# A new order for the convolutions and the gated block behind a shifted-window attention: finer split steps, more buffers, one core

## The reference, cut to what matters

```
x = x + attention(gn(x))      # shifted 7x7 windows, 8 heads, softmax
x = x + binary_conv(gn(x))    # sign(input) (*) sign(kernel), 3x3, times box-summed |gn(x)|, plus bias
x = x + ternary_conv(gn(x))   # full-precision input (*) sign(kernel), 3x3
x = x + gated(gn(x)):
    xb, z = split(x_flat @ W_in)            # 128 + 128 channels
    u = silu(causal_conv4(xb) + conv_b)     # per channel, along the 784 tokens of an image
    out = (4 * u * silu(z)) @ W_out
```

## Time and profile before

| | |
|---|---|
| median of 3 runs | 215.12 us (214.6 to 215.54) |
| the profiled execution | 215.54 us, its span 213.7 us |
| PE busy | 200.5 us (94%) |
| DVE, ACT, POOL busy | 152.2, 138.8, 91.7 us |
| attention | to about 126.8 us |
| conv stage | 126.8 to 174.3 us |
| gated block | 174.3 to 208.6 us, then its last steps and the store |

### The profile page before, as it was taken

How to read it: one execution, slowest core, us unless ns; L and a number is a source line. 1 busy time by engine, 2 the same in 40 slices (tenths; PEclk the granted TensorE clock), 3 DMA queues, 4 the chain that set the end, 5 groups by cost and what they waited for, 6 DMA issues and landing times.

```text
span 213.7 us, 6850 instructions
## 1 busy us (share of the span) xinstructions
PE 200.5 (94%) x2767; PEld 140.6 (66%) x2767; DVE 152.2 (71%) x316; ACT 138.8 (65%) x294; POOL 91.7 (43%) x103
## 2 busy tenths in 40 slices
PE   7888999999999999999999998999689899899994
PEld 2456788888888878888788875665456564545441
DVE  3585699977886868878769764989797861625543
ACT  2347697779776987788878662188445455876631
POOL 0359999730325199322792019487435410100000
PEclk9999999999999999999999999999999999999999
DMA  6970000000000000000000000001343300002022
GB/s 208 440 294 3 3 3 3 3 3 3 5 3 3 0 5 3 3 3 3 2 3 3 5 3 0 0 5 41 79 100 94 86 0 3 0 0 75 14 108 104
DMA packets 4382, 9.16 MB, mean 43 GB/s; under 512 B 641, under 2 KB 3201, under 8 KB 4225
## 3 DMA queue, kind: packets, MB, share of 16 engines
q1 hardware_dynamic: 4208, 8.41, 11.9%
q10 hardware_dynamic: 144, 0.34, 0.4%
HBM read 5.03 MB, written 1.61 MB: 31 GB/s over the span
## 4 chain that ended last, share of the span: by engine, by line
PE 71%; DVE 8%; ACT 7%; DMA 4%; issue 4%; POOL 3%; SPq 1%; ACTq 0%; DVEq 0%; POOLq 0%
PE turned L691 12%; PE outs L711 11%; PE scores L680 10%; PE scores L893 5%; PE scores L894 4%; PE qkv L651 4%; PE qkv L661 4%; PE scores L793 4%; PE turned L921 3%; PE outs L733 2%; DMA xw<-xw_in 2%; PE turned L839 2%; DMA p<-parts 2%; PE scores L911 2%; ACT pt L460 2%
## 5 line engine op out<-in xcount | busy, mean ns | idle before, releaser
L1014 DVE TENSOR_REDUCE mx<-scores 113x16 f32<-113x784 f32 x32 | 30.9, 965 | 8.3 <-PE scores L680 8.1
L691 PE MATMUL turned<-cst,d 113*113 113x113 f32 x256 | 33.3, 273 | 0.9 <-DVE d L1019 0.9
L691 PEld LDWEIGHTS turned<-cst,d 113*113 113x113 f32 x256 | 27.8, 178 | 8.5 <-issue 7.1
L460 ACT ACTIVATE pt<-turned 113x392 f32<-113x392 f32 x64 | 28.4, 495 | 7.1 <-PE turned L691 5.9
L206 POOL TENSOR_TENSOR kex<-ks,cst 128x784 f32<-128x784 f32 (+1 forms) x16 | 23.5, 1472 | 20.9 <-ACT ks L439 20.8
L1019 DVE TENSOR_TENSOR d<-scores,mx 113x784 f32<-113x784 f32 x32 | 31.2, 976 | 1.1
L711 PEld LDWEIGHTS outs<-vsb,pt 113*49 113x49 f32 x1024 | 26.1, 125 | 6.1 <-issue 2.9
L430 ACT ACTIVATE scores<-rel 113x784 f32<-113x784 f32 x32 | 26.1, 817 | 5.1 <-DMA rel<-rel_in 3.9
L711 PE MATMUL outs<-vsb,pt 113*49 113x18 f32 x1024 | 29.2, 199 | 0.0
L283 POOL TENSOR_TENSOR rstd<-ve,mhalf 128x1 f32<-128x1 f32 (+1 forms) x15 | 8.7, 577 | 46.7 <-DVE ve L980 46.6
L680 PE MATMUL scores<-kex,qs 32*49 32x196 f32 x512 | 28.2, 332 | 0.0
(11 more groups left out here) (118 smaller groups left out, 359.1 us busy)
## 6 DMA issues: line engine op xcount, KB each, us to landing
p<-parts SPq DMA_DIRECT2D x14, 112.5 KB, 2.2
x<-x_in SPq DMA_DIRECT2D x1, 1568.0 KB, 9.8
out<-res SPq DMA_DIRECT2D x8, 196.0 KB, 1.9
xw<-xw_in SPq DMA_DIRECT2D x2, 392.0 KB, 4.9
xw<-xw_in SPq DMA_DIRECT2D x1, 784.0 KB, 6.7
ker<-ker_in SPq DMA_DIRECT2D x2, 288.0 KB, 10.1
p3x<-parts SPq DMA_DIRECT2D x8, 60.0 KB, 2.0
late<-late_in SPq DMA_DIRECT2D x1, 417.0 KB, 10.8
```

The costliest lines, as they stand in the source:

```text
L460: act.activation(pt[0:WK, k % 2, j].rearrange("p n (w t) -> p n w t", w=2), ps_t[j][0:WK, :].rearrange("p (n w t) -> p n w t", n=4, w=2)[: ...
L691: mm = pe.transpose(ps_t[j][0:WK, n * P:n * P + WK], d[0:WK, k % 2, h:h + 2, :].rearrange("p a b -> p (a b)")[:, 0:WK], ident[0:WK, 0:WK])
L1014: dve.tensor_reduce(top, sc, AXX, ALU.max).then_inc(max_done, 1)
```

## The change

- On PE the last values, projections, channel sums and `conv1` steps behind the attention stand in another order; `channel_sums(3, *)` now stands ahead of the first `conv2_stacked`, and `conv2` is written out in its three steps.
- `split_a` is cut into `first_part` and `whole` (the bfloat16 part first, then `xf`); `split_b` into `second_part` and `place_second`. SP's sends are a list, with both first parts (g = 0, 1) ahead of the third part of 0.
- Conv2 has semaphores of its own (`conv2_done`, `x2_done`).
- The last three `mix` steps are `mix(col(3, 1..3))` behind `conv2_third(3)`, in the spare columns of another bank (`late_mix`); before it was two, and `mix(col(3, 1))` stood ahead of `conv2(3)`.
- `tap_weights` moves from the conv stage into step R = 8 of the attention on DVE. It also makes `wo4`, four times `wo`, so that the product is a plain multiply.
- A one-column Silu, and with it the table load, stands in ACT's program right behind the attention loop.
- `xs` holds all 4 groups, `su` and `sz` 8 halves. `yy` and `res` lie over the dead tiles `kex` and `xw`. The expands use banks 2 and 3, the gate branches 6, 7, 0 and 1 by turns.
- The gated block is interleaved by single steps on PE, ACT and DVE.
- `ON_POOL` and `BY_TAPS` are empty, so the branches for them are dead code.

The core of the diff:

```
         SHF = 3
-        xs = sb("xs", [P, 2, 2, SHF + TOK])
-        su = sb("su", [P, 4, HALF])
-        sz = sb("sz", [P, 4, HALF])
-        yy = sb("yy", [P, 4, HALF])
+        xs = sb("xs", [P, NG, 2, SHF + TOK])
+        wo4 = sb("wo4", [P, C])
+        su = sb("su", [P, 8, HALF])
+        sz = sb("sz", [P, 8, HALF])
...
+            def send_part(part, g):
                 s = g % 2
                 if g >= 2:
-                    sp.wait_ge(conv_done, 2 * NG + 2 * (g - 1))
+                    sp.wait_ge(conv2_done, 2 * (g - 1))
...
+            act.wait_ge(ld_late, 16)
+            act.activation(warm[:], warm[:], ACT.Silu).then_inc(warm_set, 1)
             evac_ka(0)
             evac_att(NR - 1)
...
             absolutes(NG - 1)
-            split_a(0)
             evac_ka(4)
+            first_part(0)
+            whole(0)
             evac_ka(5)
-            split_b(0)
-            split_a(1)
+            first_part(1)
+            whole(1)
+            second_part(0)
+            place_second()
...
+            channel_sums(0, 0)
+            values(NP - 1)
             conv1(0, 0)
-            values(NP - 1)
             project(NR - 2)
-            channel_sums(0, 0)
             gather(NR - 1)
+            channel_sums(0, 1)
+            channel_sums(1, 0)
+            project(NR - 1)
             conv1(0, 1)
...
+            conv2_third(3)
+            mix(col(3, 1), 1, nth(3, 1), late_mix)
+            gate_branch(0)
+            gate_branch(1)
+            mix(col(3, 2), 1, nth(3, 2), late_mix)
+            expand(0, 0)
+            expand(0, 1)
+            mix(col(3, 3), 1, nth(3, 3), late_mix)
+            expand(1, 0)
+            gate_branch(2)
+            contract(0)
+            gate_branch(3)
...
+                if R == 8:
+                    dve.wait_ge(ld_late, 16)
+                    tap_weights()
...
-                    dve.scalar_tensor_tensor(out=yy[:, 2 * (v % 2) + w, :], in0=su[:, u % 4], scalar=4.0,
-                                             in1=sz[:, u % 4], op0=ALU.mult, op1=ALU.mult).then_inc(y_ready, 1)
+            engine.tensor_tensor(yy[:, u % 4, :], su[:, u % 8], sz[:, u % 8], ALU.mult)\
+                  .then_inc(y_pool if v in ON_POOL else y_dve, 1)
```

More of the change, by code:

```diff
@@ L536, in split_a, with whole @@
                 act.activation(parts[:, s, 0, 1:1 + HW, 1:1 + HW], x[:, g], ACT.Identity, bias=nmr[:, j:j + 1],
                                scale=rstd[:, j:j + 1]).then_inc(p1_ready, 1)
-            def split_b(g):
-                s = g % 2
-                act.wait_ge(rem_ready, g + 1)
[L542 to L547, removed]
+            def whole(g):
+                s, j = g % 2, col(2, g)
+                free_split(g)
+                act.activation(xf[:, s], x[:, g], ACT.Identity, bias=nmr[:, j:j + 1],
+                               scale=rstd[:, j:j + 1]).then_inc(xf_ready, 1)
@@ L561, in gate_u @@
             def gate_u(u):
[L563 to L566, removed]
-            def gate_z(u):
[L570 to L573, removed]
+                v, w = u // 2, u % 2
@@ new lines, in gate_u @@
+                if v in BY_TAPS:
+                    act.wait_ge(tap_done, 7 * BY_TAPS.index(v) + 6 + w)
+                    act.activation(su[:, u % 8], su[:, u % 8], ACT.Silu, bias=ww("cb")).then_inc(su_ready, 1)
+                    return
+                act.wait_ge(u_done, 2 * (v - sum(t < v for t in BY_TAPS)) + w + 1)
+                if u >= 8:
+                    wait_product(act, u - 8)
+                act.activation(su[:, u % 8], bk[2 + w][:, 0:HALF], ACT.Silu, bias=ww("cb")).then_inc(su_ready, 1)
@@ L825, in conv2_third @@
                                            start=False, stop=(tap == NTAP - 1))
-                mm.then_inc(conv_done, 2)
-            def conv2(g):
-                for i in range(2):
-                    conv2_stacked(g, i)
-                conv2_third(g)
+                mm.then_inc(conv2_done, 2)
             def channel_sums(g, i):
@@ new lines, in expand @@
+                pe.wait_ge(xs_back[g], 2)
+                last = [t for t in range(v) if t not in BY_TAPS]
+                if last:
+                    pe.wait_ge(su_ready, 2 * last[-1] + w + 1)
+                else:
+                    pe.wait_ge(x2_done, 2 * NG)
+                t = xs[:, g, w]
+                pe.matmul(bk[2 + w][:, 0:HALF], g12[:, w, 0], t[:, SHF + a:SHF + a + HALF], start=True, stop=False)
+                pe.matmul(bk[2 + w][:, 0:HALF], g12[:, w, 1], t[:, SHF - 2 + a:SHF - 2 + a + HALF],
@@ L942, in _ @@
-            for w in range(2):
-                expand(2 * NG - 1, w)
-            contract(2 * NG - 2)
-            contract(2 * NG - 1)
+            pe.wait_ge(w1_ready, 2)
+            pe.wait_ge(w2_ready, 2)
+            pe.wait_ge(ld_late, 16)
+            pe.wait_ge(g12_ready, 1)
+            channel_sums(0, 0)
+            values(NP - 1)
+            conv1(0, 0)
+            project(NR - 2)
+            gather(NR - 1)
+            channel_sums(0, 1)
+            channel_sums(1, 0)
+            project(NR - 1)
@@ L947, in _ @@
+            contract(2)
+            expand(4, 0)
+            gate_branch(5)
+            contract(3)
+            expand(4, 1)
+            gate_branch(6)
+            expand(5, 0)
+            expand(5, 1)
+            contract(4)
+            expand(6, 0)
+            contract(5)
+            expand(6, 1)
+            gate_branch(7)
+            expand(7, 0)
+            expand(7, 1)
+            contract(6)
+            contract(7)
         @block.vector
```

399 lines of the change are left out of this document (230 added, 169 removed).

## The result

The changed kernel takes 218.94 us (median of 4 runs, 217.56 to 219.1), against 215.33 us for the kernel before beside it. The ratio is 1.0151, with a 95% interval of 1.0094 to 1.0209: **slower by 1.5%**, above the range that I gave. The profiled execution took 219.1 us.

What follows compares the result with a forecast made beforehand. PE's program was taken as the bound nearly everywhere. The conv stage ending at 171.5 plus a gated block of 36.25 gave 207.7 in place of 208.6, so 214.1 us on the median; range 212.0 to 216.2.

Steps and rivals of the forecast that it cites:

- The step that failed: Attention: moving `tap_weights` onto DVE there costs 0 to 1.0 us, taken as 0.
- my second: Conv stage: POOL and DVE hold each other up, box sums end at 150.5, PE loses 1.5 us; 215.6 us, chance 0.12.
- The conv stage: Conv stage ends at 171.5 instead of 174.3, 2.8 us earlier, of which 0.5 us is a mix that comes back later.
- the projection's wait: Start of the conv stage: PE's 1.0 us wait ahead of a projection goes, putting everything behind it 1.0 us ahead.
- DVE's order: Conv stage: `signs(3)` and `remainder(0)` behind the variances of (2, 1) help the last box sum end at 149.0, not 151.18.
- the wait for the parts of conv2(3): Conv stage: of PE's 0.8 us wait for the DMA of the parts, 0.4 us stays; conv2(3) starts at 166.7.
- 2.4 us of waits: Conv stage: PE waits the forecast left in place, from 4.8 us less 2.35.
- The gated block: Gated block takes 36.25 us, from 34.3: 2.05 us more for run edges, 0.57 less wait, 0.47 of mix.
- rival 1: Gated block cuts are free, or most remaining conv-stage waits vanish: 2.05 us better, 212.1 us; chance 0.13.
- rival 3: Gated block: lone expands or contracts pay double at edges, 4.1 us for 11 more runs, 216.2 us; chance 0.14.
- The table load: Behind the attention on ACT: the 1.28 us load and 0.2 us Silu move without a price; cover 0.6 us.
- rival 4: Behind the attention: the table switch costs 1.4 us beyond its row, last projection some 0.7 us late; 214.8 us, chance 0.06.

Runs made afterwards that it cites:

- c2: Changed kernel with the scaling of `wo` alone left at R = 8 and the four tap products moved to R = 6; 213.72 us.
- a2: Changed kernel with all of `tap_weights` (products and scaling) at R = 6 in place of R = 8; 213.73 us.
- a4: Changed kernel with 30 filler matmuls on zeros ahead of the transposes that wait in the attention; 216.76 us.
- b2: a2 with `signs(3)` and `remainder(0)` back ahead of the variances of (2, 1) on DVE; 216.81 us.
- b3: a2 with PE's old order at the end of the attention, `conv1(0, 0)` back ahead of the last values; 214.9 us.
- b1: a2 with the gated block in longer runs on PE, ACT and DVE ordered to match; 212.03 us.
- a1: Changed kernel with the tap products back in the conv stage and the scaling of `wo` taken out; 213.72 us.
- a3: Kernel before with only `tap_weights` moved to R = 8 and the unused scaling of `wo` added; 219.52 us (218.52 and 220.51).
- c3: b2 with eight filler matmuls on zeros ahead of `mix(col(2, 2))`; 215.29 us.

## Why the prediction was wrong, point by point

**The step that failed** is what it said of `tap_weights`: "It costs from 0 to 1.0 us; I take 0, since DVE's share is far from full and PE's is." It cost 5.2 us (218.94 less 213.73). The amount of work was right: 0.89 + 0.19 us, and at R = 6 or 9 it costs no more than in the conv stage (213.73, 213.72 and 213.72 us). The reason given was wrong. A busy share over 25 us says nothing of what another engine does in that one microsecond, and R = 8 is a step in which POOL makes box sums. The views of before had it: the box sums run at this place too, and the prediction itself quotes `remainder` at 1.84 us beside POOL and 0.92 alone. The products have two inputs in SBUF, as `remainder` has. The chain, each link with its row or run:

1. Some instructions of DVE are held until POOL's instruction in flight has ended: the products, the scaling and `remainder` among them, whose inputs all lie in SBUF. Those that read PSUM are not (c2). The line of the products, in the kernel after and in a2 (duration in ns: least, median, most):

```profile
L1191 DVE TENSOR_TENSOR g<-late x4: 279/530/1935, 78.8 to 81.5; 128x128 f32<-128x128 f32 x4
```

```profile
L1191 DVE TENSOR_TENSOR g<-late x4: 281/284/285, 63.9 to 64.5; 128x128 f32<-128x128 f32 x4
```

   The same four instructions are all alike at 281 to 285 ns in a2. In the kernel after, two are free (0.28 us each), one takes 0.78 us, until `kex` on POOL has ended, and one 1.94 us, until the first box sum has (the median, 530 ns, lies midway between 0.28 and 0.78 us). The Trainium skill, SBUF — State Buffer, Who interferes with whom, says of this that DVE shares its second pair of ports with GpSimd, that an instruction with two SBUF inputs or in a 2-port mode contends for it, and that the one that comes second "fully blocks". The trace agrees for the products. That the scaling ran in a 2-port mode no run shows; that it was held, the 1.84 us do.
2. DVE is 3.8 us late (4.88 us for 1.08 us of work). The order leaves some 2 us of slack, and PE waits 1.78 and 0.28 us: 2.3 us at the end of the attention (a4).
3. After that idle time TensorE is granted half its clock for 6.8 us ((1 - 0.984) x 217.0 = 3.5 us of full clock): 3.1 us more (a4; 2.2 by the medians). I had priced waits by their length alone.

The rival with the right mechanism was my second, POOL and DVE hold each other. I put it in the conv stage, at 1.5 us and with 0.12. There it is small: in a2 remainder(0) is not held (0.97 us) but holds POOL, whose `rstd` and `nmr` beside it take 0.80 and 0.45 us, in b2 0.55 and 0.19. These 0.5 us stand ahead of the last box sum, for which PE waits 0.8 us. third_part(0) is held by that box sum (1.82 us from 147.73 on) and PE does not wait for it.

**The conv stage**, forecast 2.8 us shorter. From the last but one values to its end it takes 44.9 us; before it took 48.3 us (174.3 less 125.97, the start of the same values in before), so 3.4 us shorter. The two orders are worth what the steps said: the projection's wait 1.0 us (b3: 1.2), DVE's order 1.2 us of box sum (b2), with the last one ending at 148.7 (a2) where 149.0 was forecast. What is left was 0.6 us too dear. 0.4 us of it is the wait for the parts of conv2(3), which did not come at all; the other 0.2 us was gained ahead of conv2(1), which starts 29.8 us behind those values where it started 31.9 us behind them, 2.1 us earlier for the forecast 1.9. My sum also left 2.4 us of waits and named only 1 and 0.4 of them; the trace has 1.6 us of idle time in the stage (45.00 less 43.37). The 0.5 us of waiting for signs, which I had not named, is part of it; it stands ahead of the 0.8 us for the box sum, which would be longer without it. My 5.8 us from the first send to the matmul held one slow landing, which the trace of before shows:

```profile
165.48 3.90 DMA p<-parts
```

The other transfers for conv2(3) landed in 2.2 to 2.3 us. In the kernel after all of them do, and conv2(3) starts 5.3 us behind the first send without a wait.

**The gated block**, forecast 36.25 us, took 35.8. There is no wait in it; all its loss is edges, as said. About half of an edge is there behind a `mix` as well, with no change of shape (0.77 us for 0.66), so the change of shape, to which I put the whole of it, can account for the other half at most. The size was a little high: 35.8 less 34.2 (33.73 of work and 0.47 of mix) is 1.6 us for 11 runs, 0.15 us each, where I had 0.15 to 0.2. b1 has it the other way round, 0.18 us a run. That a cut is free (rival 1) and that it pays double (rival 3) are both out.

**The table load**, forecast hidden with a cover of 0.6 us: in the kernel after ACT's next needed instruction comes 0.46 us after it was free. The load stands at 133.53 for 1.28 us and the first Silu at 134.82, so no drain shows behind it (rival 4 is out).

**Sum without the failed step.** a1 and a2 are 1.7 us below before where I said 1.0. In the profiled spans it is 2.1 us (213.7 to 211.6), of which 0.6 us is the conv stage and 0.4 us the gated block being better than forecast. Of the signs of being wrong that I had named, one came of itself: an attention that ends later than 126.9, and it made all that follows later.

## What to carry to other kernels

Before moving work on DVE into idle time, look at what POOL does in that very microsecond, not at DVE's share over a stretch. An instruction of 0.2 or 0.3 us whose inputs lie in SBUF can cost the rest of POOL's instruction beside it, not its own time; here those that read PSUM did not. Price a wait of the matmul engine not by its length alone: look in the clock column behind it, and keep cheap matmuls or other work for a place where a wait of nearly 2 us can't be avoided. And cut runs of like matmuls only where a wait asks for it; here finer steps cost 1.8 us and hid nothing that the added buffers had not already hidden.

## What I had not expected of the hardware

- The scaling, with one SBUF input, was held as well (0.19 us alone, 1.84 beside a box sum, 0.68 beside `kex`), and so was an instruction with two SBUF inputs on one column (0.80 us at 142.59 in a2, where its like takes 0.21). Not every instruction on SBUF is: the two L1060 of the moments at 146.00 in a2 take 1.04 us together beside a box sum, as the two at 140.01 do beside another step of POOL and as `BATCH_NORM_STATS2` did in before.
- POOL gives a little too: its box sums took 1.98 us each beside the held instructions, and 1.85 us where DVE had nothing of the kind (c2).
- The halved clock costs more than the wait that it follows: 3.1 us behind 2.1 us of waiting. It also comes and goes between executions of one kernel. Of 58 executions of the kernel before that ran beside the experiments, 24 had a mean clock of 0.990 to 0.992 and mostly took some 1.1 us longer (middle values about 216.3 and 215.2 us) than the 33 at full clock; one more, at 0.856, took 229.42 us. The traces show a wait of PE of 1.7 us or more in the kernel before, after, a3 and b2. After, a3 and b2 had a lowered clock in each of their 13 executions. The nine other kernels, in which the longest wait past 80 us is 1.0 us (b3's) or is filled (a4, c3), had it in 2 of 66. So part of what the new order gives may be that it takes away the long wait: against the executions of before at full clock, a2 gains 1.5 us, not 1.7. That is argued, since where the clock falls in such an execution of before no trace shows.
